# Two quantization steps of a post-norm transformer layer move from VectorE to ScalarE

## The reference, cut to what matters

```python
x = _layernorm(x + attn(x, WQ, WK, WV, WO))
x = _layernorm(x + ffn(x, w_int8, weight_scale, bias))

def ffn(x, w_int8, weight_scale, bias):
    x_norm = x * rsqrt(mean(square(x)) + 1e-6)
    absmax = max(abs(x_norm))
    scale = 127.0 / clip(absmax, 1e-5)
    x_q = clip(round(x_norm * scale), -128.0, 127.0) / scale
    return x_q @ (w_int8 * weight_scale).T + bias
```

## Time and profile before

| | us |
|---|---|
| median of 3 runs | 1721.62 |
| lowest and highest | 1721.39, 1781.78 |
| profiled execution, its own time | 1726.41 |
| its span, slowest core (core 6) | 1724.4 |
| spans of the eight cores | 1704.7 to 1724.4 |

### The profile page before, as it was taken

One profiled execution on the slowest core, in us unless ns is written; L12 is line 12 of the kernel. 1 busy time (PEld: TensorE's weight loads), 2 busy tenths in 40 slices (PEclk: granted clock), 3 DMA queues, 4 the chain that ended last, 5 costly groups with the idle time before them and its releaser, 6 DMA issues.

```text
span 1724.4 us, 25407 instructions; the slowest of 8 cores (1704.7 to 1724.4 us)
## 1 busy us (share of the span) xinstructions
PE 1237.3 (72%) x8710; PEld 583.9 (34%) x8710; DVE 575.6 (33%) x1645; ACT 852.6 (49%) x1188; POOL 302.6 (18%) x599
## 2 busy tenths in 40 slices
PE   1899777877777775666409997877777777756664
PEld 0344333433344332222204443334443434322221
DVE  1000332221111148788600012322111111588876
ACT  0232224777788733444403322156777878334444
POOL 1000222322211111111210002232222121111112
PEclk9999876577778788888759997765677877888887
DMA  9331102000000001222192220020000000022211
GB/s 159 60 50 23 27 1 49 2 2 1 2 2 1 1 25 63 73 79 80 62 164 43 49 49 1 1 49 2 2 1 1 1 2 1 25 74 74 74 62 62
DMA packets 21918, 64.55 MB, mean 37 GB/s; under 512 B 1315, under 2 KB 1315, under 8 KB 21796
## 3 DMA queue, kind: packets, MB, share of 16 engines
q0 software_dynamic: 17184, 46.14, 12.9%
q1 hardware_dynamic: 4612, 16.78, 3.3%
HBM read 75.50 MB, written 16.78 MB: 54 GB/s over the span
## 4 chain that ended last, share of the span: by engine, by line
PE 39%; ACT 20%; DVE 14%; POOL 10%; issue 9%; DMA 5%; DVEq 1%; ACTq 0%; POOLq 0%
ACT PT L478 19%; PE psall L269 13%; POOL PT L503 9%; PE psall L314 8%; PE psall L636 8%; DMA wslotA<-wqt 5%; PE psall L377 4%; PE psall L395 3%; DVE dump L674 2%; DVE dumpb L677 2%; PE psall L421 2%; DVE st L680 1%; PE psall L821 1%; DVE st L681 1%; DVE z L838 1%
## 5 line engine op out<-in xcount | busy, mean ns | idle before, releaser
L478 ACT ACTIVATE PT<-psall,ebias 128x1024 bf16<-128x1024 f32 x448 | 468.2, 1116 | 309.2 <-PE psall L377 309.1
L377 PE MATMUL psall<-QT,KT 64*128 64x512 bf16 (+3 forms) x1280 | 280.8, 449 | 127.0 <-ACT PT L478 112.3
L395 PE MATMUL psall<-Vx,PT 128*128 128x65 bf16 x4352 | 301.9, 215 | 86.0 <-POOL PT L503 84.5
L503 POOL TENSOR_TENSOR PT<-PT,mask 128x128 bf16<-128x128 bf16 x512 | 200.6, 425 | 703.7 <-ACT PT L478 703.4
L395 PEld LDWEIGHTS psall<-Vx,PT 128*128 128x128 bf16 x4352 | 209.9, 110 | 247.1 <-issue 236.2
L540 DVE RECIPROCAL rinv<-psall 128x4 f32<-128x4 f32 x64 | 11.7, 183 | 636.8 <-PE psall L395 636.8
L636 PE MATMUL psall<-wslotA,OT 128*128 128x512 bf16 x512 | 157.2, 478 | 87.0 <-DVEq L842 87.0
L269 PE MATMUL psall<-xT,wslotA 128*128 128x512 bf16 x512 | 115.1, 389 | 87.5 <-DMA wslotA<-wqt 87.5
L327 DVE CAST Vx<-psall 128x512 bf16<-128x512 f32 x64 | 44.3, 692 | 384.4 <-PE psall L314 384.4
L821 PE MATMUL psall<-wslotB,qT 128*128 128x512 bf16 x512 | 125.2, 401 | 45.1 <-ACT qT L805 45.1
L314 PE MATMUL psall<-wslotA,xT 128*128 128x512 bf16 x512 | 147.5, 458 | 0.0
(11 more groups left out here) (93 smaller groups left out, 885.1 us busy)
## 6 DMA issues: line engine op xcount, KB each, us to landing
xstg<-x SPq DMA_DIRECT2D x32, 512.0 KB, 3.6
y<-outst POOLq DMA_DIRECT2D x32, 512.0 KB, 3.1
xT<-xt POOLq DMA_DIRECT2D x8, 1024.0 KB, 21.2
wslotA<-wqt POOLq DMA_DIRECT2D x2, 2048.0 KB, 42.0
wslotB<-wkt POOLq DMA_DIRECT2D x2, 2048.0 KB, 52.4
wslotA<-wvt POOLq DMA_DIRECT2D x2, 2048.0 KB, 15.7
wslotB<-w8t POOLq DMA_DIRECT2D x2, 2048.0 KB, 15.8
wslotA<-wot POOLq DMA_DIRECT2D x2, 2048.0 KB, 14.4
```

What stands on the lines that cost most here:

```text
L377: last = eng.matmul(out, lhsT, rhs, start=True, stop=True, skip_group_check=True)
L395: last = eng.matmul(out, lhsT, rhs, start=(i_glob < 2), stop=(i_glob >= n_total - 2), skip_group_check=True)
L478: eng.activation(PT[:, pt * 1024:(pt + 1) * 1024], psall[:, p * 1024:(p + 1) * 1024], AF.Exp, bias=ebias[:, :], scale=0.125).then_inc(sem_ ...
L503: last = eng.tensor_tensor(blk, blk, mask01[:, :], ALU.mult)
```

## The change

`VC` keeps only the clip. Its affine step and its rounding move to ACT into a new function `SBq`, as three activations with the function Identity, each behind a drain: scale and bias of the row, plus 12582912, minus 12582912. The two constants get columns of their own, filled by two memsets. `SBq(t)` is called right after `SB(t)`, and waits for `VD(t-2)`'s first step, which reads the same half of `x1b2`. `VC` now waits for `SBq` and not for `SA`.

```diff
+        rcol = small("rcol", [128, 1], F32)
+        nrcol = small("nrcol", [128, 1], F32)
...
+                eng.memset(rcol[:, :], RC)
+                eng.memset(nrcol[:, :], -RC)
...
+            def SBq(t):
+                W("s", "v", o3v.get(t - 2))
+                c0 = 14 * (t % 4)
+                def f6b(eng, t=t, c0=c0, z=zq(t)):
+                    eng.drain()
+                    eng.activation(x1b2h(t), z[:, :], AF.Identity,
+                                   bias=sc[:, c0 + 12:c0 + 13],
+                                   scale=sc[:, c0 + 7:c0 + 8])
+                    eng.drain()
+                    eng.activation(x1b2h(t), x1b2h(t), AF.Identity,
+                                   bias=rcol[:, :], scale=1.0)
+                    eng.drain()
+                    eng.activation(x1b2h(t), x1b2h(t), AF.Identity,
+                                   bias=nrcol[:, :],
+                                   scale=1.0).then_inc(sem_s, 1)
+                emit("s", f6b)
+                appd2[t] = bump("s")
+
             def VC(t):
-                W("v", "s", rsd[t])
+                W("v", "s", appd2[t])
                 W("v", "t", qtmm_v.get(t - 2))
-                c0 = 14 * (t % 4)
-                def f7(eng, t=t, c0=c0, z=zq(t)):
-                    eng.tensor_scalar(x1b2h(t), z[:, :],
-                                      sc[:, c0 + 7:c0 + 8],
-                                      sc[:, c0 + 12:c0 + 13],
-                                      ALU.mult, ALU.add)
-                    eng.drain()
-                    eng.tensor_scalar(x1b2h(t), x1b2h(t), RC, -RC,
-                                      ALU.add, ALU.add)
-                    eng.drain()
+                def f7(eng, t=t):
                     eng.tensor_scalar(qih(t), x1b2h(t), 127.0,
                                       -128.0, ALU.min,
                                       ALU.max).then_inc(sem_v, 1)
...
                 SB(t)
+                SBq(t)
                 VC(t)
...
                     SB(i + 2)
+                    SBq(i + 2)
                     VC(i + 2)
```

More of the change, by code:

```diff
@@ L595, in ph45 @@
             stats2v = {}
+            appd2 = {}
             NP = 16
```

## The result

| | before | after |
|---|---|---|
| median | 1725.8 us (10 runs) | 1883.9 us (10 runs) |
| profiled execution | 1726.4 us | 1884.1 us |
| spans of the cores | 1704.7 to 1724.4 us | 1864.7 to 1882.4 us |

Three of the ten runs of each kernel were in the chip's slower state, 0.8 to 3.3% above the others; without them the medians are 1725.7 and 1883.6 us, and the ratio leaves them out. It is 1.0916, interval 1.09 to 1.0932: slower by 9.2%. The prediction said 1871 us, 8.7% over the 1721.6 known then, with a range of 1855 to 1888, and slower with a chance of 0.96.

What follows compares the result with a forecast made beforehand. The prediction took the DVE-PE loop through L636 as the bound, replaced by a DVE-ACT loop. Entries, iterations and ends added 74.0 + 75.1 = 149.1 us to 1726.4, giving 1875.5; less 4.8 for the runs' median, 1871, range 1855 to 1888.

Steps and rivals of the forecast that it cites:

- What bounds the kernel: In ph45's regular iterations, DVE waits for PE's L636 in a loop of 14.00 us; DVE is not the bound.
- What DVE loses: VC's affine step and rounding with drains, 1.66 us per tile, worth nothing in the loop because L666 waits for PE.
- What ACT gains: Three activations with drains after SB's L749; from its start to the clip's start 5.07 us.
- The new loop: ph45's regular iterations: the clip waits for SBq, queued behind SD on ACT; period 18.75 us, adding 57.2 and 57.0 us.
- The entries: Start of ph45, tiles 0 and 1: the clip comes 3.21 us later for each, 6.4 us per batch.
- The ends: End of ph45, VD(12) to VD(15): 31.1 us per batch, adding 10.4 and 11.7 us.
- A: Rival: SBq runs in ACT's holes before L722 and L872, so not slower, about 1718 us; chance 0.03.
- B: Rival: DVE is the bound and relieving it saves 53 us over 32 tiles, giving 1669 us; chance 0.01.
- C: Rival: SBq's activations cost more through a larger drain or a table load per tile, 1912 us; chance 0.03.
- D: Rival: ACT overlaps more, 4.66 us to the clip, 13 us less, 1858; counted within the forecast's 0.93 as lower edge.

Runs made afterwards that it cites:

- clip_only: The kernel before without the affine step and the rounding, the clip reading z and nothing replacing them; 1719.2 us, ratio 0.9981.
- split_norm: The kernel before with VA and VD each cut in two, the next tile's L838 directly after L666, then VD's statistics, then VA's; 1700.7 us, ratio 0.987.
- early_sbq: The changed kernel with SBq issued one iteration ahead of its clip and x1b2 given four buffers; 1738.8 us, ratio 1.009.

## Why the prediction was right

What bounds the kernel: right, shown from two sides. clip_only took the work off DVE and gained 3 us; split_norm took PE's L636 off the loop and gained 22.

What DVE loses: "worth nothing" in the loop, right.

What ACT gains, 5.07 us from SB's activation to the clip: measured 5.15 (1636.03 to 1641.18). The two in-place activations took 1.15 and not L874's 1.13, and from the end of the last one (1641.01) to the clip there were 0.17 and not 0.10; the rest agreed to 0.02.

The new loop, 18.75 us: most iterations took 18.83, the mean was 18.94. Nine of the 24 took 19.1 to 19.2; each has a single extra gap of some 0.3 us, between two of DVE's own instructions or ahead of the clip. What these gaps are is open. That makes +118.7 us for the 24 iterations against 114.2.

The entries, 6.4 us each: 6.5 and 6.7 measured.

The ends, 31.1 us each: 32.4 and 32.5 measured. For its size this term is the most wrong, 24.7 for 22.1, though the loop missed by more microseconds, 118.7 for 114.2. I allowed for PE's lower clock in L821 only. The transposes ahead of it took it too:

```profile
922.99 0.69 DVE L783 TENSOR_SCALAR qint<-x1b 128x1024 bf16<-128x1024 f32 x1 [7.85 <-ACT x1b L773]
...
923.83 1.01 PE L806 MATMUL psall<-ident,qint 128*128 128x128 bf16 x8 [4.69 <-DVE qint L783]
...
926.15 5.78 PE L835 MATMUL psall<-wslotB,qT 128*128 128x512 bf16 x16 [1.31 <-ACT qT L819]
932.10 1.28 DVE L852 SCALAR_TENSOR_TENSOR z2x<-psall,w2a,x1b 128x1024 f32<-128x1024 f32 x1 [5.02 <-PE psall L835]
```

L806 took 1.01 and not 0.61 us, L835 started 2.32 and not 1.91 after it, and took 5.78 and not 5.0. From clip to L852 are 9.11 us where 8.0 were taken. The mean granted clock from 922 to 932 us was 0.66.

Term by term the sum is 13.1 + 118.7 + 24.7 = 156.6 against 12.8 + 114.2 + 22.1 = 149.1. The forecast of 1871 also started from a median of 1721.6; over ten runs the kernel before has 1725.8. These two, 7.5 and 4.2 us, are the 12.9 us between forecast and result, but for 1.2. No error cancelled another: every term came out larger than it was taken, and the result lies in the upper part of the range, 4 us below its end.

The rivals. A (the work hides): not so in the changed kernel, where L783 waits 7.85 us, and the prediction's reason held, that each engine takes its queue in order: the same work hides in early_sbq's iterations once its place in the queue is another. (A's time of 1718 is a middle value; four times 1.66 us would give 1715 at the lowest.) B (DVE is the bound, 1669 us) is refuted by clip_only. It becomes true only in split_norm's order, where shedding the same work gained a further 26 us on the same chip (1700.7 to 1674.6). C (larger activations, or a table load per tile): L727 has two loads in the whole profile, as L722 had, none stands between the activations, and they took 1.24 and 1.15 us. D, the overlap at 4.66 us, did not come.

The Trainium skill ("Perfetto Trace Analysis", section "Optimizing Scalar/DVE Operations") says that offloading some work to Scalar may make sense if DVE is saturated. The runs bear out the condition. With DVE 82% busy but waiting for PE, offloading cost 9%; with DVE as the bound (87% busy) and the activations ahead of need, it gained 1.5% (0.987 to 0.972).

## What to carry to other kernels

Before moving work to a half-idle engine, write down what stands ahead of it in that engine's queue: the receiver waits for all of it, and here that place alone cost 87 of 158 us. A relief of the busiest engine is worth nothing while a wait on another engine follows right behind it; remove that wait first (split_norm), then move the work, and issue it an iteration ahead of its use, which took two more buffers here. The early issue alone was no gain (early_sbq, 0.9% slower than before); it paid only with the other wait gone.

## What the runs showed of the hardware that I had not expected

The slow matmuls changed place. Before, L636 took 4.94 us for its sixteen matmuls and L821 3.61. After, it is the other way: PE sits idle ahead of the transposes (4.86 and 7.04 us in the rows below), these and L835 run slow, and L641 right behind them takes 3.61. The mean granted clock is 0.56 from 1622.84 to 1631.30 us and 1.00 from 1631.37 to 1635.00.

```profile
1622.84 1.01 PE L806 MATMUL psall<-ident,qint 128*128 128x128 bf16 x8 [4.86 <-DVE qint L783]
1625.16 6.13 PE L835 MATMUL psall<-wslotB,qT 128*128 128x512 bf16 x16 [1.31 <-ACT qT L819]
1631.37 3.61 PE L641 MATMUL psall<-wslotA,OT 128*128 128x512 bf16 x16
1642.02 1.01 PE L806 MATMUL psall<-ident,qint 128*128 128x128 bf16 x8 [7.04 <-DVE qint L783]
```

The mean granted clock of the iterations fell from 0.86 to 0.73 of full speed. Within the iterations it cost nothing, since DVE did not wait for PE there.

Twice in clip_only, at the end of each batch, DVE's clip took 2.24 us in place of 0.69. In batch 0 it started at 839.07, while POOL's addition of two 128x1024 operands ran (838.62 to 840.75), and so in batch 1:

```profile
839.07 2.24 DVE L761 TENSOR_SCALAR qint<-z2x 128x1024 bf16<-128x1024 f32 x1 [0.24 <-issue]
...
1693.35 2.23 DVE L761 TENSOR_SCALAR qint<-z2x 128x1024 bf16<-128x1024 f32 x1 [0.24 <-issue]
```

```profile
838.62 2.13 POOL L771 TENSOR_TENSOR x1b<-x,bias_b 128x1024 f32<-128x1024 bf16 x1 [0.21 <-ACT x L749]
...
1692.90 2.13 POOL L771 TENSOR_TENSOR x1b<-x,bias_b 128x1024 f32<-128x1024 bf16 x1 [0.20 <-ACT x L749]
```

The first ended 0.56 us after POOL's. All eight cores show it, twice each, at 2.23 to 2.25 us; these sixteen are the only clips of that run that overlap an addition of POOL, and no clip, rounding or affine step of DVE in any other run does. DVE's L666 (1.22 to 1.23 us, one of its two wide inputs in PSUM) and L674 (1.22 us) did run beside POOL's addition at their usual length. This fits the Trainium skill's note ("Perfetto Trace Analysis", section "Optimizing Scalar/DVE Operations") that GpSimd and DVE share a read port of SBUF. Why the port would hold the clip and not these two, no run here tests.
